# Rounded halves for the projections of groups 2 to 7, and routing in units of two groups, in a gated cross-attention and expert kernel

## What is computed

```python
def _L0_xattn_ref(x, y, pad_mask, Wq, Wkv):          # 16 heads of 16
    q = (x @ Wq.T).reshape(B, N, H, d).transpose(0, 2, 1, 3)
    kv = (y @ Wkv.T).reshape(B, N2, 2, H, d).transpose(2, 0, 3, 1, 4)
    k, v = (kv[0], kv[1])
    attn = jnp.einsum('bhnd,bhmd->bhnm', q * scale, k)
    attn = jnp.where(pad_mask[:, None, :, None], attn, jnp.float32(-1000000000.0))
    attn = jax.nn.softmax(attn, axis=-1)
    out = jnp.einsum('bhnm,bhmd->bhnd', attn, v)

def _L0_ffn_ref(hidden_states, w_router, fc1_w, fc2_w, gate_w, up_w, down_w):
    logits = x @ w_router
    top_logits, top_idx = jax.lax.top_k(logits, TOPK)       # 2 of 8
    scores = jax.nn.softmax(top_logits, axis=-1)
    ...
    for e in range(E):
        h1 = permuted * m @ fc1_w[e]
        proj, gate = jnp.split(h1, 2, axis=-1)
        out_perm = out_perm + jax.nn.silu(proj) * gate @ fc2_w[e]
    ...
    shared = jax.nn.silu(hidden_states @ gate_w) * (hidden_states @ up_w) @ down_w
    return moe_out + shared

x = x + jnp.tanh(g_xattn[0]) * _L0_xattn_ref(_layernorm(x), ctx_768, mask, Wq, Wkv)
x = x + jnp.tanh(g_ffn[0]) * _L0_ffn_ref(_layernorm(x), w_router, fc1_w, fc2_w, gate_w, up_w, down_w)
```

## Time and profile before

| | us |
|---|---|
| median of 3 runs | 344.53 |
| lowest, highest | 343.54, 345.41 |
| the profiled execution | 344.35 |
| its span | 342.6 |
| busy: PE, DVE, ACT, POOL | 313.0, 251.3, 170.8, 120.0 |

### The profile page before, as it was taken

The page is one execution under the profiler, slowest core; times in us unless marked ns, Lnnn a source line. Parts: engine busy times, 40 slices in busy tenths (PEclk is TensorE's granted clock), DMA queues, the critical chain, the costliest instruction groups (busy, mean ns, idle before and its releaser), DMA issues.

```text
span 342.6 us, 8091 instructions
## 1 busy us (share of the span) xinstructions
PE 313.0 (91%) x2484; PEld 257.1 (75%) x2484; DVE 251.3 (73%) x777; ACT 170.8 (50%) x325; POOL 120.0 (35%) x133
## 2 busy tenths in 40 slices
PE   8878989988889885878999999999999999999986
PEld 7656767877777774755547488888898888888875
DVE  5557578899989897886789936666676666643795
ACT  2533766766666572546781326444444454423131
POOL 5731111217171716056440062843433433431000
PEclk9958999999999996789999999999999999999999
DMA  8896596766566555211135001333333333202951
GB/s 236 240 230 187 167 238 206 176 181 197 170 196 187 159 173 170 96 65 62 46 106 147 13 15 50 99 96 101 101 108 89 95 96 96 72 27 82 420 175 61
DMA packets 34917, 46.52 MB, mean 136 GB/s; under 512 B 5599, under 2 KB 29539, under 8 KB 34370
## 3 DMA queue, kind: packets, MB, share of 16 engines
q1 hardware_dynamic: 27714, 28.51, 29.1%
q10 hardware_dynamic: 3712, 8.98, 8.2%
q0 software_dynamic: 3456, 8.56, 7.3%
HBM read 21.55 MB, written 12.62 MB: 100 GB/s over the span
## 4 chain that ended last, share of the span: by engine, by line
PE 55%; DVE 16%; SPq 9%; DMA 8%; issue 6%; POOL 3%; ACT 2%; ACTq 0%; POOLq 0%; DVEq 0%
PE ps L1612 26%; SPq L354 5%; PE ps L1289 4%; DVE mx L901 4%; DMA stacks<-work 3%; PE ps L1337 3%; DVE x_all L1248 3%; PE ps L1354 3%; SPq L361 3%; PE ps L1662 2%; PE ps L1584 2%; PE ps L1490 2%; PE ps L1387 2%; PE ps L1604 2%; POOL dispatched L494 2%
## 5 line engine op out<-in xcount | busy, mean ns | idle before, releaser
L539 POOL DMA_INDIRECT expert_rows<-v_s,slot_u x39 | 38.3, 981 | 62.7 <-ACT v_s L806 48.1
L901 DVE TENSOR_REDUCE mx<-ps 128x8 f32<-128x1024 f32 x32 | 39.2, 1224 | 12.1 <-PE ps L1354 11.6
L502 POOL TENSOR_TENSOR work<-work 128x512 bf16<-128x512 f32 x16 | 18.5, 1155 | 60.3 <-ACT work L590 60.2
L621 ACT ACTIVATE probs<-ps 128x1024 f32<-128x1024 f32 x32 | 32.6, 1020 | 12.3 <-PE ps L1387 12.2
L1198 DVE TENSOR_TENSOR act<-ps,sil 128x256 f32<-128x256 f32 x39 | 16.6, 425 | 29.1 <-ACT sil L799 29.0
L799 ACT ACTIVATE sil<-ps 128x256 f32<-128x256 f32 x39 | 15.0, 385 | 39.5 <-PE ps L1612 39.4
L1612 PE MATMUL ps<-fc_hi,xs_hi 128*128 x78 | 34.2, 438 | 0.0
L1612 PE MATMUL ps<-fc_lo,xs_hi 128*128 x78 | 30.9, 396 | 0.0
L1612 PE MATMUL ps<-fc_hi,xs_lo 128*128 x78 | 30.8, 394 | 0.0
L1354 PE MATMUL ps<-stacks 96*128 96x128 bf16 x256 | 21.4, 231 | 8.7 <-DMA stacks<-work 4.5
L494 POOL DMA_INDIRECT dispatched<-row_s,slot_u x24 | 24.2, 1008 | 12.6 <-issue 7.0
(11 more groups left out here) (211 smaller groups left out, 810.7 us busy)
## 6 DMA issues: line engine op xcount, KB each, us to landing
stacks<-work SPq DMA_DIRECT2D x93, 128.0 KB, 2.9
xs_in<-dispatched SPq DMA_DIRECT2D x39, 129.0 KB, 2.1
fc_s<-in_fc ACTq DMA_DIRECT2D x8, 512.0 KB, 3.6
fc_s<-in_fc ACTq DMA_DIRECT2D x8, 256.0 KB, 4.1
stacks<-expert_rows SPq DMA_DIRECT2D x2, 1024.0 KB, 5.8
probs<-expert_rows SPq DMA_DIRECT2D x2, 1024.0 KB, 9.9
ctx_s<-in_ctx_t SPq DMA_DIRECT2D x8, 192.0 KB, 3.4
x_all<-in_x SPq DMA_DIRECT2D x1, 1536.0 KB, 8.3
```

Of the source, the lines that this page charges most:

```text
L502: nc.gpsimd.tensor_tensor(out[:, 2, :], rest, out[:, 1, :], ALU.subtract).then_inc(ready, 1)
L539: nc.gpsimd.indirect_dma_start(ys, bass.IndirectOffsetOnAxis(dst_u[:, r:r + 1], 0), y_out[:, r, :], None, bounds_check=2 * T - 1, oob_is_e ...
L621: nc.scalar.activation(probs[:, 2 * j + h], ps_t, ACT.Exp, scale=HD ** -0.5).then_inc(probs_ok[j][h], 1)
L901: nc.vector.reduce_max(mx[:, j, 8 * h:8 * h + 8], ps_s, AX_X).then_inc(max_ok[j][h], 1)
```

## The change

**Halves.** For groups 2 to 7 the three projections are computed as three fp32r products each, from high and low halves of the context, of the normalized tokens and of the three weights. All high halves are copies on ScalarE, all low halves subtractions on GpSimd. The low halves overwrite their fp32 originals; the high ones lie in the places of the last two experts' weights, which are therefore loaded after the last projection. The context load stands further ahead in SyncE's order. The router's weight operand has 8 columns in place of 96.

**Routing.** Groups 0 and 1, 2 and 3, and 4 and 5 form units, groups 6 and 7 one each. `logits` still runs for each group; choice, indices, positions, places and weights run once for a unit, over four blocks of 128 tokens in place of two. Groups 2 and 3 get rows of their own (`row_h`, in the place of `hid_0`). Dispatches start one pass later, and four of them are left after the loops instead of three. The running count `cum` has one column set. Behind the loops, the indices of group 6 are taken ahead of the last normalized rows.

```diff
@@ SyncE
             for s in range(2, G + 3):
                 if live(s - 3):
                     max_rows(s - 3, 0)
+                if live(s):
+                    load_ctx(s)
                 if live(s - 2) and s > 2:
                     stack_q(s - 2, 0)
                     stack_q(s - 2, 1)
                     stack_q(s - 2, 2)
                 if live(s - 3):
                     max_rows(s - 3, 1)
-                if live(s):
-                    load_ctx(s)
                 if live(s - 1):
                     stack_free(s - 1)
@@ GpSimd
+            def ctx_low(g):
+                pool.wait_ge(ctxh_ok, g - 1)
+                nc.gpsimd.tensor_tensor(ctx_lo[:, g % 2], ctx_s[:, g % 2], ctx_hi[:, g % 2].bitcast(F32),
+                                        ALU.subtract).then_inc(ctxl_ok, 1)
...
             third(1, kst, k_rest, k_ok[1], k_pc, k_ok[2])
+            weight_low(wkh_ok, k_done, wk_lo[:, :, :, :], wk_s[:, :, :, :], wk_hi[:, :, :, :], wkl_ok)
+            weight_low(wvh_ok, v_done, wv_lo[:, :, :], wv_s[:, :, :], wv_hi[:, :, :], wvl_ok)
+            ctx_low(2)
             third(1, qst, q_rest, q_ok[1], q_pc, q_ok[2])
+            weight_low(wqh_ok, q_done, wq_lo[:, :, :, :], wq_s[:, :, :, :], wq_hi[:, :, :, :], wql_ok)
             for s in range(2, G + 2):
                 if live(s - 3):
                     power2(s - 3, 0)
-                if live(s - 5):
-                    dispatch(s - 5)
+                if live(s - 6):
+                    dispatch(s - 6)
@@ ScalarE
                 if live(s - 1) and s > 2:
                     normed_t(s - 1)
+                    xn_high(s - 1)
...
                     exp(s - 3, 0, 0)
+                if s == 2:
+                    weight_high(wk_in, wk_hi[:, :, :, :], wk_s[:, :, :, :], wkh_ok)
+                    weight_high(wv_in, wv_hi[:, :, :], wv_s[:, :, :], wvh_ok)
+                    ctx_high(2)
+                    weight_high(wq_in, wq_hi[:, :, :, :], wq_s[:, :, :, :], wqh_ok)
+                if live(s) and s > 2:
+                    ctx_high(s)
                 if live(s):
                     norm1(s)
...
-                if live(s - 2):
+                if live(s - 2) and s - 2 < E - 2:
                     load_experts(s - 2)
+                if s == G + 1:
+                    sa.wait_ge(v_done, G)
+                    sa.wait_ge(q_done, G)
+                    load_experts(E - 2)
+                    load_experts(E - 1)
@@ VectorE, chosen and places
-                ve.wait_ge(cum_ok, g + 1)
-                link(nc.vector.tensor_tensor(cnt[:, :, :], oh[:, :, 0, :], oh[:, :, 1, :], ALU.add))
-                nc.vector.tensor_tensor(cum[:, 1, :], cum[:, 0, :], cnt[:, 0, :], ALU.add).then_inc(oh_ok, 1)
+                nc.vector.tensor_tensor(cnt[:, 0:n, :], oh[:, 0:n, 0, :], oh[:, 0:n, 1, :], ALU.add).then_inc(oh_ok, 1)
...
+                if g < G - 1:
+                    link(nc.vector.reduce_sum(new[:, :], cnt[:, 0:n, :].rearrange("p j e -> p e j"), AX_X))
+                    nc.vector.tensor_tensor(cum[:, :], cum[:, :], new[:, :], ALU.add).then_inc(cum_ok, 1)
@@ TensorE
+            def products(out, high, low, x_high, x_low, first, last):
+                for n, (a, b) in enumerate(((high, x_high), (high, x_low), (low, x_high))):
+                    ins = nc.tensor.matmul(out, a, b, start=first and n == 0, stop=last and n == 2)
+                return ins
...
+                if g >= 2:
+                    pe.wait_ge(xnl_ok, g - 1)
+                    if g == 2:
+                        pe.wait_ge(wql_ok, 1)
+                    for c in range(2):
+                        for k in range(2):
+                            last = products(whole[:, TG * c:TG * c + TG], wq_hi[:, k, c, :], wq_lo[:, k, c, :],
+                                            xn_hi[:, k, :], xn_lo[:, k, :], k == 0, k == 1)
+                    last.then_inc(q_done, 1)
+                    return
```

More of the change, by code:

```diff
@@ L947, in logits @@
             def logits(g):
+                at = g - units[g // 2 if g < 6 else g - 3][0]
                 ve.wait_ge(router_done, g + 1)
-                nc.vector.tensor_copy(lg[:, :, :], ps_c[:, 0:2 * NV].rearrange("p (j e) -> p j e", j=2)[:, :, 0:8]
+                nc.vector.tensor_copy(lg[:, 2 * at:2 * at + 2, :],
+                                      ps_c[:, 0:2 * NV].rearrange("p (j e) -> p j e", j=2)[:, :, 0:8]
                                       ).then_inc(lg_read, 1)
             def choice(g):
+                if g not in ended:
+                    return
@@ new lines, in weights @@
+            def weights(g):
+                if g not in ended:
+                    return
+                u, n = ended[g], 2 * len(units[ended[g]])
+                ve.wait_ge(ex_ok, u + 1)
+                link(nc.vector.tensor_scalar(den[:, 0:n, :], ex[:, 0:n, :], 1.0, None, ALU.add))
+                link(nc.vector.reciprocal(sc1[:, 0:n, :], den[:, 0:n, :]))
+                rows = rows_in_unit[u].rearrange("p (j k) c -> p j k c", k=2)
+                link(nc.vector.tensor_scalar(rows[:, :, 0, D + 1:D + 2], sc1[:, 0:n, :], tg[:, 1:2], None, ALU.mult))
+                nc.vector.tensor_tensor(rows[:, :, 1, D + 1:D + 2], rows[:, :, 0, D + 1:D + 2], ex[:, 0:n, :],
@@ L1334, in values_proj @@
                 pe.wait_ge(xnt_ok, g + 1)
+                if g >= 2:
+                    if g == 2:
+                        pe.wait_ge(wvl_ok, 1)
+                    for j in range(2):
+                        rows = slice(P * j, P * j + P)
+                        for k in range(2):
+                            last = products(ps_v[:, D * j:D * j + D], ctx_hi[:, g % 2, k, rows],
+                                            ctx_lo[:, g % 2, k, rows], wv_hi[:, k, :], wv_lo[:, k, :], k == 0, k == 1)
+                    last.then_inc(v_done, 1)
+                    return
                 for j in range(2):
@@ L1421, in tokens_t @@
                 if g:
-                    pe.wait_ge(pos_read, g)
+                    pe.wait_ge(lg_read, g)
+                if g >= 2:
+                    pe.wait_ge(pos_read, g // 2 if g < G - 1 else len(units) - 1)
                 for k in range(2):
@@ L1607, in _ @@
                         last.then_inc(down_done, 1)
-            def products(out, high, low, x_high, x_low, first, last):
-                for n, (a, b) in enumerate(((high, x_high), (high, x_low), (low, x_high))):
-                    ins = nc.tensor.matmul(out, a, b, start=first and n == 0, stop=last and n == 2)
-                return ins
             def gate_up(c, j):
```

233 lines of the change are left out of this document (149 added, 84 removed).

## The result

The changed kernel takes 354.43 us in the median of four executions (351.63 to 356.61), the kernel before 344.03 us on the same chip: a ratio of 1.0284, 95% interval 1.0236 to 1.0332, so 2.8% or 10 us slower. Forecast were 345.1 us, with a range up to 350.0 us. Single executions of one kernel scatter with the granted clock (the kernel before: 342.28 us at a mean clock of 0.980, 346.22 us at 0.964), so what single traces show is where a wait lies, not what it costs. Times go by the ratios, from which disturbed executions are left out (the profiled executions of short_proj, short_fill and before_fill are of that kind).

The account below looks back on a forecast made before the run. It took SyncE's transfer queue and landing to bound most of a stage. Terms: +3.2 +0.9 -0.8 +0.4 -1.0 -0.7 -0.3 -1.0 = +0.7 us on 344.35, giving 345.1 us; range 340.5 to 350.0 us.

Parts of the forecast that it names:

- What bounds the kernel: Group 6's attention stage: 12.1 of 16.6 us are SyncE's queue and one landing, 4.5 us compute.
- The port: VectorE's places and normalized rows beside GpSimd's subtractions: +0.9 us together, between -1.5 and +4.6.
- The term of -0.8 us: Group 4's stage: the long slot product is gone with its places, -0.8 us.
- The products: Projections of groups 2 to 7: 1.06 us a group less TensorE time, nearly nothing on the path beside transfers.
- The rival of the clock: Groups 5 and 6: less work and longer waits lower TensorE's clock, 2 x 2.2 us, 349.5 us; chance 0.12.
- Rival 4: Weights' low halves behind group 1's third key piece hold VectorE's first-maxima split: 2.4 us late, 347.5 us; chance 0.04.
- The context load: SyncE's queue, now ahead of the query transfers for five groups (loads 3 to 7): 5 x 0.65 = +3.2 us.
- Queries: Groups 2 and 3: queries wait for GpSimd's halves and the copy's delay, +0.4 us together, between 0 and 1.5.
- Keys of group 7: SyncE's key issue without an expert load just ahead: 3.9 us, -1.0 us, between 0 and -1.1.
- Dispatch: Before group 4's scores: first dispatch moves one stage on, ending a 0.70 us wait, -0.7 us, between 0 and -1.0.
- Routing in units: Two groups routed at once: slot product -0.8, dispatch -0.7, last stage -0.3, end -1.0, in all -2.8 us.
- The order at the end: Index work ahead of the last normalized rows: last transposes start near 162.8 us, -1.0 us, between 0 and -1.2.

Follow-up runs that it names:

- short_proj: Kernel before with one of the four fp32 matmuls of each projection left out in groups 2 to 7: ratio 1.0094 to before.
- short_fill: short_proj plus useless fp32 matmuls ahead of the query-transfer waits of groups 4 to 7 and group 6's second maxima: ratio 1.0004 to before.
- before_fill: Kernel before plus useless fp32 matmuls ahead of the query-transfer waits of groups 4 to 7 and group 6's second maxima: ratio 1.0048.
- after_fill: Changed kernel plus useless fp32 matmuls ahead of the query-transfer waits of groups 4 to 7 and group 6's second maxima: ratio 1.0309 to before.
- ctx_ahead: Kernel before with the context load alone moved ahead of the six query transfers: ratio 1.0074 to before.
- route_only: Changed kernel without the halves: fp32 projections, old places of context and expert loads, routing in units, new order at the end: ratio 0.9951 to before.
- low_cut: Changed kernel with GpSimd's context and token subtractions cut from 512 to 16 columns a group, products reading high halves instead: ratio 1.0151 to before.
- early_low: Changed kernel with GpSimd's two low halves of a group moved ahead of the second inverse root and third key piece: ratio 1.0286 to before.
- low_on_dve: Changed kernel with the low halves of context (groups 3 to 7) and tokens (2 to 7) made by VectorE, last in its pass: ratio 1.0280.
- route_fill: route_only plus useless fp32 matmuls ahead of the query-transfer waits of groups 4 to 7 and group 6's second maxima: ratio 0.9959 to before.
- early_weights: Changed kernel with the subtractions on key and value weights moved ahead of group 1's third key piece on GpSimd: ratio 1.0328 to before.
- spare_copy: Kernel before plus two useless one-input GpSimd copies of 128x512 fp32 a stage, where the changed kernel has its low halves: ratio 1.0068.

## Why the prediction was wrong, point by point

- **What bounds the kernel.** The division of a stage into SyncE's part and 4.5 us of compute was right. SyncE's part came to +2.2 us, against +3.2 - 1.0 - 0.7 + 0.4 = +1.9 us forecast, but by luck: the stages of groups 2 to 7 changed by +0.9, +1.5, +0.45, +0.6, -1.3 and 0.0 us, and several of the terms are not where they were put (below). The miss is in the compute part, +6.4 us, and in the start, +3.0 us.
- **The port: the step that failed.** "I take -0.1 and +0.6 each, between the ends as I have no row nearer to one": +0.9 us, at most +4.6. The subtractions cost 6.8 us (4.5 to 9.0) alone in the kernel before, and 4.6 us (0 to 9) when taken out of the changed kernel, so the upper end may have been too low too. It let VectorE be held once in a stage without places, for 1.2 us, which less the 0.8 us of the places that are gone made the bound of 0.4; in group 3's stage each of the two rows is held by one subtraction, 2.67 - 0.73 = 1.9 us. The places of the units stand in the stages of groups 4 and 6 (slot products at 93.25 and 128.70 us), not of 5 and 7. The term of -0.8 us was misplaced as well: the long slot product of 69.03 us lies in group 3's stage, and in group 4's it is not gone but takes 1.29 us. And it looked at the slot product and the rows alone, where any difference, cast or scaling between SBUF tensors can be held.
- **The products.** Their length was right, "nearly nothing on the path" was not: TensorE's shorter work by itself costs 3.2 us. The rival of the clock has the mechanism that short_proj's trace shows, in the stages of groups 5 and 6 that it named. In the changed kernel the stages of groups 4 to 6 are no shorter at full clock (after_fill); there the lower clock shows ahead of group 2's keys and of the last transposes.
- **The weights' halves.** Rival 4, with a chance of 0.04, is what the trace shows at 28.34 us: two steps held, 2.0 us. What that costs in the end no run shows. As a rival to the others it was misplaced, since nothing kept it from coming with them.
- **The context load.** 2.5 us against 3.2: right in size. The sum had 0.65 us in each of five stages; in ctx_ahead's trace group 5's stage has none of it and group 4's has more.
- **Queries.** They wait 1.47 us in group 2. In group 3, where 1 us and more was forecast, they do not wait, nor after.
- **Keys of group 7.** Their issue takes 3.80 us, as forecast, but the 1.0 us did not reach the path: the part from freeing to first scores is 12.1 us as before, since the last query transfer, issued 1.1 us sooner, took that much longer to land. And an expert load just ahead is no sure sign of a slow issue: the kernel before has one 2.4 us ahead of group 6's keys too, which take 3.82 us.
- **Dispatch.** The 0.70 us wait ahead of group 4's scores did not go, it is 1.35 us.
- **Routing in units.** -2.8 us forecast, -1.7 us (-3.5 to +0.1) measured alone, and -2.5 us with a wider interval beside the halves. The order at the end came as forecast; route_only, TensorE at the last transposes, which answers to the earlier trace rows:

```profile
159.92 0.18 PE L1564 MATMUL ps<-cnt,before 128*128 128x8 bf16 x1
...
160.56 0.63 PE L1536 MATMUL ps<-ident,row 128*128 128x128 f32 x4 [0.36 <-DVE slot L1047]
```

  The 0.92 us wait ahead of the positions is gone. In the changed kernel the gain does not show: from group 7's freeing to the last transposes it takes 41.5 us, against 41.0 before and 39.5 in route_only; 1.1 of the 2.0 us over route_only are the four matmuls at 170.60 us.
- **The sum.** The parts done alone give 6.8 + 3.2 + 2.5 - 1.7 = 10.8 us, the change 9.8 us: they add up within their intervals. This supports the account and does not prove it: low_cut's interval is wide, early_low and low_on_dve changed the held work and left the ratio, and nothing shows that the 3.2 us of short_proj are lost in the changed kernel too. The forecast's rivals were priced as alternatives, with 2 in 10 for two of one sign together; parts of three of them (port, clock, weights' halves) came together.

The version to keep is the routing in units without the halves, route_only at 0.9951 and route_fill at 0.9959 (0.9923 to 0.9995): some 0.4% under the kernel before, at the edge of what these runs can tell.

## What to carry to other kernels

Work that GpSimd does between SBUF tensors is not free where VectorE is busy: price it at its whole length on VectorE until a run shows less, and ask which of VectorE's operations then waits, not whether the two or three that you know of do. Less work for TensorE ahead of a wait can cost time (3.2 us here), probably because the clock falls in the longer wait. And risks with causes of their own should be added in a range, not set against each other.

## What the runs showed of the hardware

- VectorE operations of a few elements (128x4 in early_low, 128x12 in early_weights) take 1.20 and 1.22 us beside a GpSimd subtraction of 1.27 and 1.26 us. Reductions from PSUM are not held: the maxima take 1.21 to 1.23 us in all traces, beside GpSimd or not.
- Between two GpSimd subtractions that stand back to back VectorE gets in one operation, and is then held by the second (75.19 us: two rows, 2.67 us); the second subtraction took 1.37 us there and 1.29 us elsewhere.
- GpSimd copies of one input hold VectorE too: two rows take 1.37 us beside two copies of 0.65 us each (spare_copy, 106.86 us), 0.73 alone.
- The issue of the same six key transfers takes 3.82 us at 106.02 and 4.91 us at 122.78 us in the kernel before, each with an expert load issued 2.4 us ahead.
